# Quantised cross attention: queries on partitions and a turn of the weights, against keys on partitions with four heads at a time

## The chip, the cores and the metric

The kernel runs on one core of a Trainium2 chip. The metric is the device time of one execution in microseconds (us), the median of several runs. Nothing else runs on the core.

## The reference

Four gated layers work on x (2048 rows of 512). Each adds tanh(gate) times a cross attention and tanh(gate) times a feed-forward part. The change is in the attention of the second layer, whose 16 heads of 32 channels let 2048 queries look at 2048 keys:

```python
q = _fq_sym(q * scale, axis=-1)            # steps of max|q| / 127, per row and head
k = _fq_sym(k, axis=-1)
v = _fq_sym(v, axis=2)                     # per channel, over the keys
attn = softmax(einsum('bhqd,bhkd->bhqk', q, k))
s = max(attn over keys) / 255
attn = clip(round(attn / s), 0, 255) * s   # unsigned, per query row
out = einsum('bhqk,bhkd->bhqd', attn, v)
x = x + tanh(g) * (out @ Wp + bp)
```

The largest weight of a row becomes 255, so a kernel needs the largest score of each row before it can round any weight of it. With it, exp(score - top + ln 255) rounded to a whole number is the quantised weight, and the sum of the unrounded exponentials divides the result.

## The kernel before

The program is a row of stages, each a block in which all five engines have an instruction list of their own; a stage ends with a barrier of all engines. PSUM has 8 banks of 128 x 512 f32. TensorE (PE) multiplies, VectorE (DVE), ScalarE (ACT) and GpSimd (POOL) work on tiles, SyncE (SP) issues the DMAs. The second layer's attention is this row of stages in `layer1_xattn`: weights split in two f16 parts, keys projected and quantised (`quantised_heads` with `parts=kT`), values (`quantised_values`), then weights, `transposed_parts` and `quantised_heads` for the queries, `attention_quantised`, and last the output projection: weights (`split_weights`), `transposed_parts` of the output o, and `project_and_add`.

`quantised_heads` has two forms. With `ints` (the queries) it keeps whole numbers in one f16 array and the steps in sq. With `parts` (the keys) it multiplies back by the step (L1307), and ACT (L1331) and POOL (L1319) split the product in a high and a low f16 part; both are turned on PE.

`attention_quantised` goes head by head, 16 tiles of 128 queries each, so 256 tiles. For a tile, PE computes the scores twice. The first time (L1512, four matmuls of 512 keys) only DVE reads them, for the row's largest score (L1617, combined in L1621, made a shift in L1625). The second time (L1505, four matmuls) ACT takes exp with scale and shift, two instructions of 1024 keys, written as 16-bit whole numbers, with their sums (L1586). Queries are on partitions there, but the product with the values needs keys on partitions. So PE turns the weights in 16 pieces (L1517), DVE copies half of them out of PSUM (L1630) and ACT the other half (L1592); the whole numbers are read as f16 bit patterns. Then 16 matmuls of 32 columns give the output (L1525), which DVE copies to o (L1635). POOL divides by the sums once per head (L1496 to L1498). The order on each engine is written by hand; the rings are three deep over tiles.

The attention of the third layer (`attention_clipped`, L2198 to L2297) and of the fourth (`attention_causal`, L2714 to L2933) already work with keys on partitions. PE multiplies keys by queries at 128 x 512, ACT takes exp as f32, and the products with the values (L2212, L2806) and with ones (L2215, L2806) are f32 matmuls of 32 columns. Four of these, at four groups of 32 output partitions, run side by side. In the trace each f32 matmul is two instructions.

## Time and profile before

| | us |
|---|---|
| median of 3 runs | 3355.14 (3348.61 to 3356.6) |
| profiled execution, its own time | 3352.55 |
| its span in the profile | 3350.5 |
| attention stage, first POOL instruction to last | 870.4 to 1794.3 |

| engine | busy us | share of span |
|---|---|---|
| PE | 2675.5 | 80% |
| DVE | 2482.1 | 74% |
| ACT | 1909.9 | 57% |
| POOL | 602.2 | 18% |

The shares are means over stages that have different limits. The attention stage is over a quarter of the span, and in it PE, DVE and ACT are all busy for over nine tenths of the time, while POOL has almost nothing to do. The times of the profiled execution are used for all working; it is 2.6 us below the median of the runs.

### The profile page before, as it was taken

Reading aid. Unit: us, or ns where it says so; the run is one execution under the profiler, and the core shown is the slowest. Engines: PE = TensorE matmul, PEld = TensorE weight load, DVE = VectorE, ACT = ScalarE, POOL = GpSimd, SP = SyncE. Lnnn points to the kernel's source line nnn. Section 1 sums busy time; section 2 is a strip of 40 time slices with the busy share of each in tenths; the row PEclk is TensorE's granted clock in tenths of the full one; section 3 lists DMA queues with packets and bytes.
Section 4 is the critical chain, followed back from the end, with each engine's and each line's share of the span. In section 5 each row is a group of like instructions: output and inputs, shape, how many; then the busy total and the mean of one; then the engine's idle time right before and its main releaser. Section 6 shows DMA issues by size and latency. Waiting matters only on the chain. (4 is left out here: it accounts for less than half of the span.)

```text
span 3350.5 us, 62405 instructions
## 1 busy us (share of the span) xinstructions
PE 2675.5 (80%) x21148; PEld 1391.2 (42%) x21148; DVE 2482.1 (74%) x4757; ACT 1909.9 (57%) x2773; POOL 602.2 (18%) x539
## 2 busy tenths in 40 slices
PE   4868999686799999999996777776698756759983
PEld 3444444333365656565663433333311132224542
DVE  5756677666799999999995666634299798986548
ACT  2554433232499999999995433331387534845541
POOL 4440000012100010101013233312111260030013
PEclk7988999897899999999998888888799877869996
DMA  4433420200000000000000200010133010031301
GB/s 151 174 145 121 151 77 38 91 0 16 19 13 7 13 7 13 7 13 8 7 1 16 88 1 0 0 63 16 44 86 82 26 51 0 1 101 39 66 8 54
DMA packets 65338, 151.98 MB, mean 45 GB/s; under 512 B 11840, under 2 KB 20048, under 8 KB 63376
## 3 DMA queue, kind: packets, MB, share of 16 engines
q1 hardware_dynamic: 62368, 140.43, 14.1%
q0 software_dynamic: 2800, 9.18, 0.8%
q8 instruction: 119, 1.95, 0.2%
q14 instruction: 51, 0.42, 0.0%
HBM read 93.61 MB, written 24.38 MB: 35 GB/s over the span
## 5 line engine op out<-in xcount | busy, mean ns | idle before, releaser
L1617 DVE TENSOR_REDUCE s_top<-ps 128x1 f32<-128x512 f32 x1024 | 656.2, 682 | 30.3 <-PE ps L1512 30.0
L1586 ACT ACTIVATE s_prob<-ps,s_shift,m_sq 128x1024 int16<-128x1024 f32 x512 | 614.7, 1201 | 29.9 <-DVE s_shift L1625 29.9
L1512 PE MATMUL ps<-s_ks,s_qs 128*128 128x512 f16 x1024 | 352.5, 386 | 60.6 <-issue 14.1
L1517 PEld LDWEIGHTS ps<-ident,s_prob 128*128 128x128 f16 x4096 | 272.2, 98 | 123.1 <-DVE m_o L1635 52.3
L1517 PE MATMUL ps<-ident,s_prob 128*128 128x128 f16 x4096 | 313.8, 220 | 0.7 <-ACT s_prob L1586 0.5
L1505 PE MATMUL ps<-s_ks,s_qs 128*128 128x512 f16 x1024 | 306.5, 381 | 0.8 <-ACT s_prob L1586 0.5
L1592 ACT ACTIVATE s_probT<-ps 128x1024 f16<-128x1024 int16 x256 | 261.9, 1023 | 5.8 <-PE ps L1517 4.8
L1008 PE MATMUL ps<-m_hT,m_w 128*128 128x512 f16 x1024 | 231.8, 381 | 1.8 <-PEq L105 1.8
L249 PE MATMUL ps<-ident,s_parts 128*128 128x128 f16 x640 | 75.5, 290 | 130.0 <-POOL s_parts L240 128.1
L2289 DVE TENSOR_SCALAR s_prob<-ps,s_cap 128x1024 f32<-128x1024 f32 x128 | 158.2, 1269 | 25.4 <-PE ps L2198 25.3
L1630 DVE CAST s_probT<-ps 128x1024 f16<-128x1024 int16 x256 | 174.1, 680 | 3.4 <-PE ps L1517 3.4
L2912 DVE TENSOR_REDUCE s_ntop<-ps 128x1 f32<-128x512 f32 (+3 forms) x256 | 107.3, 482 | 87.2 <-PE ps L2772 87.2
L2233 ACT ACTIVATE s_prob<-s_prob 128x1024 f32<-128x1024 f32 x128 | 131.1, 1051 | 58.6 <-DVE s_prob L2289 55.6
L1059 ACT ACTIVATE s_silu<-ps,scale 128x512 f32<-128x512 f32 x64 | 43.9, 685 | 205.3 <-PE ps L1008 205.3
L1496 POOL TENSOR_TENSOR s_sums<-s_z 128x16 f32<-128x16 f32 x16 | 3.5, 217 | 833.5 <-DVE m_o L1635 833.5
L1008 PEld LDWEIGHTS ps<-m_hT,m_w 128*128 128x128 f16 x1024 | 100.5, 98 | 123.8 <-issue 2.2
L1512 PEld LDWEIGHTS ps<-s_ks,s_qs 128*128 (+1 forms) x1024 | 80.4, 96 | 167.5 <-DVE s_top L1617 108.1
L2212 PE MATMUL ps<-s_prob,m_values 128*32 128x512 f32 x512 | 136.0, 610 | 13.0 <-ACT s_prob L2233 12.8
L1525 PE MATMUL ps<-s_hv,s_probT 128*128 128x32 f16 x4096 | 142.2, 176 | 1.7 <-ACT s_probT L1592 1.7
L2883 ACT ACTIVATE s_prob<-ps 128x384 f32<-128x384 f32 (+1 forms) x192 | 89.5, 516 | 86.0 <-PE ps L2795 85.8
L2215 PE MATMUL ps<-s_prob,s_ones 128*32 128x512 f32 x512 | 136.0, 610 | 0.0
L1525 PEld LDWEIGHTS ps<-s_hv,s_probT 128*128 128x128 f16 x4096 | 129.5, 96 | 2.2 <-issue 2.2
(407 smaller groups left out, 5622.4 us busy)
## 6 DMA issues: line engine op xcount, KB each, us to landing
s_qs<-m_qT SPq DMA_DIRECT2D x144, 128.0 KB, 2.5
s_ks<-m_kT SPq DMA_DIRECT2D x96, 128.0 KB, 2.4
numbers<-s_numbers SPq DMA_DIRECT2D x21, 512.0 KB, 3.0
s_slabs<-numbers SPq DMA_DIRECT2D x21, 512.0 KB, 4.4
m_ks<-context_parts SPq DMA_DIRECT2D x12, 512.0 KB, 7.5
expert_rows<-s_y SPq DMA_DIRECT2D x19, 256.0 KB, 2.0
s_rows_in<-in_ctx SPq DMA_DIRECT2D x16, 256.0 KB, 3.0
x_sb<-in_L_ffn_W_up SPq DMA_DIRECT2D x4, 1024.0 KB, 7.2
```

Source lines behind the costliest of these rows:

```text
L1008: i = pe.matmul(k.ps[:, 2 * (n % 2) + j, :], wt[:, c, cols(n, P)], hT[:, l, c, cols(g, GT)], start=(l == c == 0), stop=(l == 1 and c == DC ...
L1505: j = pe.matmul(pair(half)[:, m, :], qs[:, hb, bass.ds(t * P, P)], ks[:, hb, cols(2 * half + m, 512)], start=True, stop=True)
L1512: pe.matmul(quarter_at(q), qs[:, hb, bass.ds(t * P, P)], ks[:, hb, cols(q, 512)], start=True, stop=True).then_inc(s.top_scored, 1)
L1517: j = pe.transpose(turned(half, F16)[:, cols(m, P)], prob[:, u, cols(8 * half + m, P)].bitcast(F16), k.ident[:])
L1525: j = pe.matmul(output, probT[:, u, m, :], hv[:, hb, m, :], start=(m == 0), stop=(m == T - 1))
L1586: act.activation(prob[:, u, cols(half, HALF)], pair(half).rearrange("p m n -> p (m n)"), ACT.Exp, bias=shift[:, u:u + 1], scale=sq[:, bass ...
L1592: act.activation(probT[:, u, 8:16, :].rearrange("p m n -> p (m n)"), turned(1, I16), ACT.Copy).then_inc(s.half1_copied, 1)
L1617: dve.tensor_reduce(top4[:, u, q:q + 1], quarter_at(q), AX.X, ALU.max).then_inc(s.top_read, 1)
L1630: dve.tensor_copy(probT[:, u, 0:8, :].rearrange("p m n -> p (m n)"), turned(0, I16)).then_inc(s.half0_copied, 1)
L2212: pe.matmul(values_at(m)[cols(j, HD), :], values[:, b * KT + t, 2 * pair + j, :], prob[:, n % R, j, :], start=(t == 0), stop=(t == KT - 1))
L2215: i = pe.matmul(sums_at(m)[cols(j, HD), :], ones[:], prob[:, n % R, j, :], start=(t == 0), stop=(t == KT - 1))
L2289: dve.tensor_scalar(prob[:, n % R, :, :], k.ps[:, 2 * (n % A):2 * (n % A) + 2, :], cap[:, tile:tile + 1], -LIMIT, ALU.min, ALU.max).then_i ...
```

## The change

`attention_quantised` is written anew, with keys on partitions. A block is four heads (one 128-partition chunk of the channels) by 512 queries; there are 16 blocks (BLOCKS), each with 16 key tiles (KT) of 128 keys, so 256 steps. In a step, each of the four heads a has:

- one score matmul, 128 keys by 512 queries (`score`, L1574), and one exp of it on ACT, 128 x 512, written as f32 (L1619);
- one cast of these weights to 16-bit whole numbers on POOL (`tensor_copy`, L1528);
- a share of two groups of four 32-column matmuls side by side: values times the whole numbers read as f16 (`mix_values`, L1583), and ones times the f32 weights (`mix_ones`, L1590). Both lag the scores by two steps.

Both groups add up in PSUM over the block's 16 steps, in bank 6 and bank 7. The turning of weights (16 pieces a tile), the copies out of PSUM and the read-outs per tile go.

The largest scores are still taken with queries on partitions: four matmuls a step (`top`, L1557) and four DVE reductions (L1651), 19 steps ahead (AHEAD), in three banks of their own. Since queries are now in the free dimension, the shift can't be a bias of ACT. DVE makes three f16 parts of the least negated top for the block's 16 tiles (L1657 to L1661), PE turns them (L1564), DVE copies them (L1668), and a DMA puts them in 5 more rows of the queries, against 5 rows of 16 in the keys. So the score matmul has 96 + 5 rows. Three DMAs a head load the queries of a block (`queries`, 12 a block) and the keys of four blocks (`keys`). Queries are stored with their step multiplied in and in two parts, as the keys are: `quantised_heads` runs with `parts=qT` for them, three combinations of parts are stacked in the 96 rows, and the separate factor sq goes. Where `quantised_heads` had one multiplication of two tensors (and for queries one more for the scale), it has one scalar_tensor_tensor.

At a block's end ACT copies both sums out (L1625, L1626). SP stores the four rows of sums to DRAM, loads them as 128 rows of 16, DVE inverts those (L1672), and SP stores them and loads them again spread over 32 partitions a head. POOL multiplies (L1533), ACT makes the high part (L1630), POOL the low part (L1537), directly in qT and already in the layout that `project_and_add` reads. So o and the stage `transposed_parts(k, oT, tiles=o)` go. The loops are written out: nothing is a hardware loop in this stage.

On PE, in the middle of the attention stage, a tile before (ks and qs are stacked keys and queries, prob the weights, probT the turned weights, hv a head's values) is:

```order
L1512 MATMUL ps<-s_ks,s_qs 128x512
L1511 REGISTER_ALU
L1512 MATMUL ps<-s_ks,s_qs 128x512
L1533 ISA
L1505 MATMUL ps<-s_ks,s_qs 128x512 x2
L1536 REGISTER_ALU
L1517 MATMUL ps<-ident,s_prob 128x128 x8
L1525 MATMUL ps<-s_hv,s_probT 128x32 x16
```

and the other half of the tile has the same again without the last row. A step now (ints are the whole numbers, ones a tile of one value) is:

```order
L1574 MATMUL ps<-s_qs,s_ks 128x512
L1557 MATMUL ps<-s_ks,s_qs 128x512
L1583 MATMUL ps<-s_ints,m_values 32x512 x4
L1574 MATMUL ps<-s_qs,s_ks 128x512
L1557 MATMUL ps<-s_ks,s_qs 128x512
L1590 MATMUL ps<-s_prob,s_ones 32x512 x4
L1574 MATMUL ps<-s_qs,s_ks 128x512
L1557 MATMUL ps<-s_ks,s_qs 128x512
L1574 MATMUL ps<-s_qs,s_ks 128x512
L1557 MATMUL ps<-s_ks,s_qs 128x512
```

Eight full matmuls remain of eight; 16 turns and 16 matmuls of 32 columns became two groups of four, each entered from a full matmul and left to one.

On DVE, the rows between the reductions of one block and of the next (ntop are the negated tops, compact the sums as 128 rows of 16) are now:

```order
L1651 TENSOR_REDUCE s_ntop<-ps 128x1 x64
L1657 TENSOR_REDUCE s_least<-s_ntop 128x16
L1658 TENSOR_SCALAR s_shift<-s_least 128x16
L1659 SCALAR_TENSOR_TENSOR s_rest<-s_least,s_shift 128x16
L1660 TENSOR_SCALAR s_shift<-s_rest 128x16
L1661 TENSOR_TENSOR s_shift<-s_rest,s_shift 128x16
L1651 TENSOR_REDUCE s_ntop<-ps 128x1 x4
L1668 COPY s_shiftT<-ps 80x128
```

Five dependent small instructions stand between two reductions once a block; before, a small pair stood there once a tile.

On ACT, the copies at a block's end stand behind the exps of the next block's second step:

```order
L1619 ACTIVATE s_prob<-ps 128x512 x72
L1625 ACTIVATE s_sums<-ps 128x512
L1626 ACTIVATE s_num<-ps 128x512
L1619 ACTIVATE s_prob<-ps 128x512 x40
L1630 ACTIVATE m_qT<-s_num 128x512
```

72 exps are 18 steps, so the first copy waits for the last matmul of step 15 with the exps of steps 16 and 17 already ahead of it.

The diff, cut to its core:

```diff
@@ -1292,11 +1292,9 @@
                     v.done(dve.reciprocal(inv[:], step[:, u, :]))
-                    if scale != 1.0:
-                        v.done(dve.tensor_scalar(inv[:], inv[:], scale, None, ALU.mult))
-                    v.done(dve.tensor_tensor(scaled[:, u, :].rearrange("p (h d) -> p h d", d=HD),
-                                             rows[:, u, :].rearrange("p (h d) -> p h d", d=HD),
-                                             inv[:].unsqueeze(2).broadcast_to([P, H, HD]), ALU.mult))
+                    v.done(dve.scalar_tensor_tensor(scaled[:, u, :].rearrange("p (h d) -> p h d", d=HD),
+                                                    rows[:, u, :].rearrange("p (h d) -> p h d", d=HD), scale,
+                                                    inv[:].unsqueeze(2).broadcast_to([P, H, HD]), ALU.mult, ALU.mult))
...
@@ -1416,254 +1414,273 @@
-def attention_quantised(k, qT, sq, kT, values, o):
...
+def attention_quantised(k, qT, kT, values):
...
+    SHIFTS = 5
...
+    A = H // DC
+    ROWS = 3 * HD
...
+    STEPS = BLOCKS * KT
+    TILES = A * TG
+    AHEAD = KT + 3
+    LAG = 2
+    EVACUATE, INVERT, DIVIDE, HIGH, LOW = 1, 6, 9, 11, 11
+    END = STEPS + KT
...
+        qs = s.sb("qs", [P, 3, A, GT], F16)
+        ks = s.sb("ks", [P, 2, A, N], F16)
+        prob = s.sb("prob", [P, 4, A, GT], F32)
+        ints = s.sb("ints", [P, 3, A, GT], I16)
...
+        mixed_at, sums_at = k.ps[:, 6, :], k.ps[:, 7, :]
...
+            def spread_inverse(b):
+                sp.wait_ge(s.evacuated, 2 * b + 1)
+                sp.dma_start(k.inverse[0, :, :], sums[0:P:HD, :]).then_inc(s.sums_stored, 16)
+                sp.wait_ge(s.sums_stored, 16 * (b + 1))
+                sp.dma_start(compact[:], k.inverse[0, :, :].rearrange("a (j e) -> (a j) e", j=HD)).then_inc(s.sums_loaded, 16)
+                sp.wait_ge(s.inverted, b + 1)
+                sp.dma_start(k.inverse[1, :, :].rearrange("a (j e) -> (a j) e", j=HD), compact[:]).then_inc(s.inverse_stored, 16)
+                sp.wait_ge(s.inverse_stored, 16 * (b + 1))
+                for a in range(A):
+                    sp.dma_start(sums[cols(a, HD), :], k.inverse[1, a, :].partition_broadcast(HD)).then_inc(s.inverse_spread, 16)
+            for b in range(BLOCKS):
+                sp.wait_ge(s.top_read, number["shift", b] + 1)
+                sp.dma_start(qs[ROWS:ROWS + SHIFTS, b % 3, :, :], shiftT[:, b % 2, :]).then_inc(shifted[b % 3], 16)
+                if b and b + 2 < BLOCKS:
+                    sp.wait_ge(s.scored, A * KT * b)
+                    for a in range(A):
+                        queries(b + 2, a, q_loaded[(b + 2) % 3])
+                if b and b % G == 0 and b // G + 1 < DC:
+                    for a in range(A):
+                        keys(b // G + 1, a, k_loaded[(b // G + 1) % 2])
+                if b:
+                    spread_inverse(b - 1)
+            spread_inverse(BLOCKS - 1)
...
+            pool.memset(ks[ROWS:ROWS + SHIFTS, :, :, :].rearrange("p u a n -> p (u a n)").bitcast(F32), TWO_SIXTEENS
+                        ).then_inc(s.consts_ready, 1)
+            for n in range(STEPS + KT):
+                if n < STEPS:
+                    if n >= 3:
+                        pool.wait_ge(s.values_mixed, n - 2)
+                    for a in range(A):
+                        pool.wait_ge(s.exp_ready, A * n + a + 1)
+                        pool.tensor_copy(ints[:, n % 3, a, :], prob[:, n % 4, a, :]).then_inc(s.rounded, 1)
+                if n >= KT and n % KT == DIVIDE:
+                    b = n // KT - 1
+                    pool.wait_ge(s.inverse_spread, 16 * A * (b + 1))
+                    pool.wait_ge(s.evacuated, 2 * (b + 1))
+                    pool.tensor_tensor(num[:], num[:], sums[:], ALU.mult).then_inc(s.divided, 1)
+                if n >= KT and n % KT == LOW:
+                    b = n // KT - 1
+                    pool.wait_ge(s.hi_ready, b + 1)
+                    pool.tensor_tensor(qT[:, 1, b // G, cols(b % G, GT)], num[:], qT[:, 0, b // G, cols(b % G, GT)],
+                                       ALU.subtract).then_inc(s.lo_ready, 1)
...
+            def bank_free(job):
+                if job >= 3:
+                    pe.wait_ge(s.top_read, job - 2)
+            def top(i, q):
+                b, a, tile = i // TILES, i % TILES // TG, i % TG
...
+                job = number["top", i, q]
+                bank_free(job)
+                pe.matmul(top_at(job), qs[0:ROWS, b % 3, a, cols(tile, P)], ks[0:ROWS, c % 2, a, cols(q, GT)],
+                          start=True, stop=True).then_inc(s.top_scored, 1)
+            def turn_shift(b):
+                job = number["shift", b]
+                bank_free(job)
+                pe.wait_ge(s.shift_ready, b + 1)
+                pe.transpose(k.ps16[0:SHIFTS * TILES, job % 3, 0:P], shift[:, b % 2, :, :].rearrange("p l i -> p (l i)"),
+                             k.ident[:]).then_inc(s.top_scored, 1)
+            def score(n, a):
+                b, t = n // KT, n % KT
+                g = A * n + a
+                if t == a == 0:
+                    pe.wait_ge(shifted[b % 3], 16 * (b // 3 + 1))
+                if g >= 3:
+                    pe.wait_ge(s.exp_ready, g - 2)
+                pe.matmul(score_at(g), ks[0:ROWS + SHIFTS, b // G % 2, a, cols(t, P)], qs[0:ROWS + SHIFTS, b % 3, a, :],
+                          start=True, stop=True).then_inc(s.scored, 1)
+            def mix_values(n):
+                b, t = n // KT, n % KT
+                if t == 0 and b:
+                    pe.wait_ge(s.evacuated, 2 * b)
+                pe.wait_ge(s.rounded, A * (n + 1))
+                for a in range(A):
+                    j = pe.matmul(mixed_at[cols(a, HD), :], values[:, t, cols(b // G * A + a, HD)],
+                                  ints[:, n % 3, a, :].bitcast(F16), start=(t == 0), stop=(t == KT - 1))
+                j.then_inc(s.values_mixed, 1)
+            def mix_ones(n):
+                t = n % KT
+                for a in range(A):
+                    j = pe.matmul(sums_at[cols(a, HD), :], ones[:], prob[:, n % 4, a, :],
+                                  start=(t == 0), stop=(t == KT - 1))
+            for m in range(-AHEAD, END):
+                i = m + AHEAD
...
+                for a in range(A):
+                    if 0 <= m + 1 < STEPS:
+                        score(m + 1, a)
+                    if i < STEPS:
+                        top(i, a)
+                    if a == 0 and LAG <= m < STEPS + LAG:
+                        mix_values(m - LAG)
+                    if a == 1 and LAG <= m < STEPS + LAG:
+                        mix_ones(m - LAG)
+                if i % TILES == 0 and 0 < i <= STEPS:
+                    turn_shift(i // TILES - 1)
...
+            def exp(n, a):
+                g = A * n + a
+                if a == 0 and n >= 4:
+                    act.wait_ge(s.mixed, n - 3)
+                act.wait_ge(s.scored, g + 1)
+                act.activation(prob[:, n % 4, a, :], score_at(g), ACT.Exp).then_inc(s.exp_ready, 1)
+            def evacuate(b):
+                if b:
+                    act.wait_ge(s.lo_ready, b)
+                act.wait_ge(s.mixed, KT * (b + 1))
+                act.activation(sums[:], sums_at, ACT.Copy).then_inc(s.evacuated, 1)
+                act.activation(num[:], mixed_at, ACT.Copy).then_inc(s.evacuated, 1)
+            def hi(b):
+                act.wait_ge(s.divided, b + 1)
+                act.activation(qT[:, 0, b // G, cols(b % G, GT)], num[:], ACT.Copy).then_inc(s.hi_ready, 1)
...
+            for n in range(STEPS + KT):
+                if n < STEPS:
+                    for a in range(A):
+                        exp(n, a)
+                if n >= KT and n % KT == EVACUATE:
+                    evacuate(n // KT - 1)
+                if n >= KT and n % KT == HIGH:
+                    hi(n // KT - 1)
...
+            def tops(i):
+                b = i // TILES
+                for q in range(4):
+                    job = number["top", i, q]
+                    dve.wait_ge(s.top_scored, job + 1)
+                    dve.tensor_reduce(ntop[:, b % 2, i % TILES, q:q + 1], top_at(job), AX.X, ALU.max, negate=True
+                                      ).then_inc(s.top_read, 1)
+            def shifts(b):
+                dve.wait_ge(s.top_read, number["top", TILES * (b + 1) - 1, 3] + 1)
+                hi, mid, lo = (shift[:, b % 2, r, :] for r in range(3))
+                v.done(dve.tensor_reduce(least[:], ntop[:, b % 2, :, :], AX.X, ALU.min))
+                v.done(dve.tensor_scalar(hi, least[:], 1.0 / SIXTEEN, None, ALU.mult))
+                v.done(dve.scalar_tensor_tensor(rest[:], least[:], 1.0 / SIXTEEN, hi, ALU.mult, ALU.subtract))
+                v.done(dve.tensor_scalar(mid, rest[:], 1.0, None, ALU.mult))
+                dve.tensor_tensor(lo, rest[:], mid, ALU.subtract).then_inc(s.shift_ready, 1)
+            def copy_shift(b):
+                job = number["shift", b]
+                if b >= 2:
...
+                dve.wait_ge(s.top_scored, job + 1)
+                dve.tensor_copy(shiftT[:, b % 2, :], k.ps16[0:SHIFTS * TILES, job % 3, 0:P]).then_inc(s.top_read, 1)
+            def invert(b):
+                dve.wait_ge(s.sums_loaded, 16 * (b + 1))
+                dve.reciprocal(compact[:], compact[:]).then_inc(s.inverted, 1)
+            for m in range(-AHEAD, END):
+                i = m + AHEAD
+                if i < STEPS:
+                    tops(i)
+                if i % TILES == 0 and 0 < i <= STEPS:
+                    copy_shift(i // TILES - 1)
+                if i % TILES == TILES - 1 and i < STEPS:
+                    shifts(i // TILES)
+                if m >= KT and m % KT == INVERT:
+                    invert(m // KT - 1)
...
@@ -3096,15 +3113,12 @@
...
             transposed_parts(k, hT, taken=True)
-            quantised_heads(k, hT, wq, k.i.L1_xattn_bq, scale, sq=sq[:].rearrange("p (h t) -> p t h", t=T), ints=qT)
-        o = sb("o", [P, H, T, HD], F32)
-        attention_quantised(k, qT, sq, kT, values, o)
+            quantised_heads(k, hT, wq, k.i.L1_xattn_bq, scale, parts=qT)
+        attention_quantised(k, qT, kT, values)
...
-            oT = sb2("oT", [P, 2, DC, N], F16)
             split_weights(k, k.i.L1_xattn_Wp, wp, row_factor=sv)
-            transposed_parts(k, oT, tiles=o)
-            project_and_add(k, oT, wp, k.i.L1_xattn_bp, 1)
+            project_and_add(k, qT, wp, k.i.L1_xattn_bp, 1)
...
```

## Rows read from the trace of the kernel before

**Rows 1.** Busy by engine in four stretches (from:to, length, PE, PEld, DVE, ACT, POOL, clock).
```profile
870.40:1794.40 924.00, 856.81 (x10240) 545.95 (x10240) 875.81 (x2048) 882.78 (x1281) 86.87 (x67) 0.98 0.04 10
807.50:869.70 62.20, 52.51 (x256) 23.18 (x256) 50.05 (x128) 9.55 (x16) 0.00 (x0) 0.91 0.01 5
639.60:714.60 75.00, 54.54 (x320) 26.14 (x320) 62.41 (x112) 24.78 (x32) 18.44 (x16) 0.93 0.05 18
1806.20:1828.20 22.00, 11.58 (x128) 8.47 (x129) 11.06 (x16) 9.74 (x16) 17.76 (x16) 0.81 0.00 0
```

**Rows 2.** Groups by line and form, 880 to 1795 us.
```profile
L1617 DVE TENSOR_REDUCE s_top<-ps 128x1 f32<-128x512 f32 x1024 | 656.2, 682 | 30.3 <-PE ps L1512 30.0
```

**Rows 3.** Instructions in order of time, PE, one tile of the attention.
```profile
1300.00 0.89 PE L1512 MATMUL ps<-s_ks,s_qs 128*128 128x512 f16 x2
...
1303.45 0.89 PE L1512 MATMUL ps<-s_ks,s_qs 128*128 128x512 f16 x2
```

**Rows 4.** In order of time, PE, third layer's attention: one step.
```profile
2560.02 0.60 PE L2198 MATMUL ps<-s_qs,s_ks 128*128 128x512 f16 x2
2560.55 0.62 PE L2212 MATMUL ps<-s_prob,m_values 128*32 128x512 f32 x2
...
2561.01 0.60 PE L2212 MATMUL ps<-s_prob,m_values 128*32 128x512 f32 x2
...
2561.55 0.60 PE L2198 MATMUL ps<-s_qs,s_ks 128*128 128x512 f16 x2
```

**Rows 5.** In order of time, PE, query projection: twelve full matmuls in a row.
```profile
818.32 2.75 PE L1247 MATMUL ps<-m_wq,m_hT 128*128 128x512 f16 x12
```

**Rows 6.** In order of time, PE, fourth layer: a narrow f16 matmul between.
```profile
3144.45 0.28 PE L2806 MATMUL ps<-s_prob,s_ones 128*32 128x128 f32 x2
3144.59 0.22 PE L2777 MATMUL ps<-ident,s_shift 128*16 128x128 f16 x1
3144.74 0.39 PE L2792 MATMUL ps<-s_qs,m_ks 98*128 98x512 f16 x1
```

**Rows 7.** Groups by line and form, POOL, whole span.
```profile
L2274 POOL TENSOR_TENSOR s_out<-s_num,s_inv 128x512 f32<-128x512 f32 x16 | 20.3, 1269 | 126.0 <-DVE s_inv L2297 125.9
...
L2276 POOL TENSOR_TENSOR m_qT<-s_out,m_qT 128x512 f16<-128x512 f32 x16 | 18.6, 1161 | 79.2 <-ACT m_qT L2247 79.2
...
L1488 POOL COPY s_hv<-m_values 128x512 f16<-128x512 f16 x16 | 9.7, 609 | 1.0
...
L142 POOL CAST ident<-ident 128x128 f16<-128x128 f32 x1 | 0.3, 289 | 0.1
```

**Rows 8.** Groups by line and form, ACT, whole span.
```profile
L2883 ACT ACTIVATE s_prob<-ps 128x512 f32<-128x512 f32 x64 | 33.7, 572 | 0.5 <-PE ps L2795 0.4
...
L2241 ACT ACTIVATE s_sums<-ps 64x512 f32<-64x512 f32 x32 | 19.0, 593 | 2.1 <-PE ps L2215 1.3
```

**Rows 9.** In order of time, DVE and POOL, the last key tile of quantised_heads.
```profile
707.14 1.15 POOL L1319 TENSOR_TENSOR s_f<-s_rows,s_f 128x512 f16<-128x512 f32 x1 [2.97 <-ACT s_f L1331]
707.76 0.57 DVE L1291 TENSOR_SCALAR s_step<-s_amax 128x16 f32<-128x16 f32 x1
```

**Rows 10.** The same view, DVE, the last query tile.
```profile
866.36 0.17 DVE L1291 TENSOR_SCALAR s_step<-s_amax 128x16 f32<-128x16 f32 x1
```

**Rows 11.** Groups by line and form, DVE, whole span.
```profile
L1716 DVE SCALAR_TENSOR_TENSOR x_sb<-ps,gate,x_sb 128x512 f32<-128x512 f32 x16 | 12.0, 751 | 23.4 <-PE ps L1686 23.4
...
L1297 DVE TENSOR_TENSOR s_scaled<-s_rows,s_inv 128x512 f32<-128x512 f32 x32 | 22.1, 692 | 1.2
```

**Rows 12.** In order of time, start and end of the attention stage.
```profile
870.41 5.21 POOL L1479 MEMSET s_qs<- 64x6144 f16 x1 [65.71 <-POOLq L105]
...
881.87 1.01 PE L1512 MATMUL ps<-s_ks,s_qs 128*128 128x512 f16 x2 [12.82 <-POOL s_hv L1488]
...
1793.28 1.05 POOL L1498 TENSOR_TENSOR m_o<-m_o,s_sums 128x512 f32<-128x512 f32 x1
```

**Rows 13.** DMA issues by line in the attention stage (KB each, us from issue to landing).
```profile
s_qs<-m_qT SPq DMA_DIRECT2D x32, 128.0 KB, 2.3
```

259 lines of the change are left out of this document (66 added, 193 removed).

## The prediction, before the changed kernel was run

> **What bounds the kernel now.** I read the busy time by stretch first. The attention stage takes 924.0 us, and PE is busy for 857, DVE for 876 and ACT for 883 of them, POOL for 87 [rows 1]. Three engines are level, so taking work from one alone would buy little. What counts is the longest engine of the new step. Next I read the instructions in order of time in mid-stage: one tile starts 3.45 us after the one before it [rows 3], and 924.0 / 256 is 3.61 with start, head changes and end. Last I looked for the new instructions where other stages already have them: the third layer's attention has full matmuls beside groups of four narrow f32 ones [rows 4], the fourth has a narrow f16 matmul [rows 6] and the 512-wide exp [rows 8].
>
> **One step on PE.** Twelve full matmuls in a row take 2.75 us, of which the last one's own latency is 0.39 [rows 5, 6], so (2.75 - 0.39) / 11 = 0.2145 us each. Eight of them, four scores and four for the tops: 1.72. In the third layer a step of two full matmuls and one f32 group of four repeats every 2561.55 - 2560.02 = 1.53 us [rows 4]. Less 0.43 for the two full ones, the group costs 1.10: 0.10 to enter, two instructions a member 0.46 apart, and the rest to leave. That is `mix_ones`. `mix_values` has f16 operands, thus one instruction a member. No row shows four narrow f16 matmuls side by side. From below: hidden switches, 0.21. From above: members one after another with both switches, 4 x 0.21 + 0.20 = 1.06. The nearest row is the narrow f16 transpose of 128 columns. It starts 0.14 us after the last f32 narrow pass, but the full matmul behind it starts 0.15 us after it, although 128 columns take only 0.054 [rows 6]. So leaving the narrow shape costs 0.10 with f16 too, and I take 0.10 + 0.21 + 0.10 = 0.42. The sum is 1.72 + 1.10 + 0.42 = 3.24 us a step on PE.
>
> The Trainium skill, TensorEngine Tiling (Array Packing), Key Properties, says that changing the tiling mode drains the engine. This case's trace agrees, with its 0.10 us on either side of a narrow group. It speaks against this change, which changes the shape four times a step where a tile before never did; by it the narrow f16 group is 0.42, not 0.21.
>
> **The other engines in a step.** DVE: 1024 reductions take 656.2 us [rows 2], 0.641 each, four are 2.56. ACT: four exps of 0.572 [rows 8] are 2.29; two copies of 0.593 and one of about 0.6 a block add 0.11: 2.40. POOL: the cast from f32 to 16-bit whole numbers is in no row. A f16 copy of 512 takes 0.609 and a f32 to f16 cast of 128 takes 0.289 [rows 7]; one slope of 0.83 ns an element and 0.18 us fixed fit both, so I take 0.61. Four are 2.44, and the multiplication (1.27) and the low part (1.16) of a block [rows 7] add 0.15: 2.59. From below 0.5 (an overlap of instructions); from above the two-input price, 1.27 [rows 7], which would make a POOL step of 5.2. PE at 3.24 is the longest, so POOL and ACT work is hidden beside it. If the cast takes over 0.77, POOL sets the step.
>
> The Trainium skill, GPSIMD Engine Reference, section 3.1, gives 769 ns measured as the best case for 512 elements of a tight loop. The 0.609 row is below that, so the measurement decides; by the page POOL would have 3.08 + 0.15 = 3.23 a step, level with PE, and the time would hardly move.
>
> **The whole stage.** PE's first matmul now waits for POOL's memset of 8192 elements a partition. 6144 took 5.21 us [rows 12], so 6.95, and with small ones before it PE starts at 870.4 + 7.5 = 877.9, four us sooner than the 881.9 of before [rows 12].
>
> - Prologue: 19 steps hold only top matmuls. DVE is the longest there: 76 x 0.641 = 48.7, plus some 1.9 for the first shift's chain: 928.5. PE and ACT can't use this time; before there was no such stretch.
> - 237 steps with tops: two without mixing at DVE's 2.57, 235 at 3.24: 766.5.
> - ACT at a block's end. The copies stand behind the exps of the second step after it and wait for `mixed` of step 15, which PE ends 2.46 us into that step (after four full matmuls and the f16 group come two passes of 0.46 and a latency of 0.60). ACT has been free since 1.8 us before. It copies for 1.11 us and only then takes the exps again. Three score banks absorb three matmuls; the fourth, due at 2.83 into the step, needs the first exp done, 2.5 + 1.15 + 0.6 = 4.25. PE stands for 1.4 us, and as it is the longest engine, that is lost: 15 blocks, 21 us.
> - DVE at a block's end: five dependent instructions. At 0.17 us for a small one [rows 10] with some 0.04 between, they take 1.1. But while POOL's two-input instruction ran, the same small one took 0.57 instead of 0.17 and ended with POOL's [rows 9, 10]. Now POOL is busy for four fifths of the time, so each of four may wait up to 0.6: 3.0 at most. The rings hide 1.2 of it. I take 2.3, a stall of 1.1 x 15 = 16 us (from 0 to 28). The turn of the shift adds 15 x 0.15 = 2.
> - 18 steps without tops at 3.24 - 0.86 = 2.38 and three with mixing only at 1.52: 47.4.
> - The end, where nothing covers the scratch chain: a copy 0.6, then store, load, inversion some 0.25 (a small DVE instruction takes 0.17 [rows 10]), store and four spreading DMAs; four landings at 2.3 [rows 13] and three more issues of 0.6 are 11.0; then 1.27, 0.6 and 1.16. Together 15.3. In the other 15 blocks POOL asks for the spread sums eight steps (26 us) after the copy. The chain has some 16 us of work, its DVE instruction stands at step 6, and POOL's casts run over one step ahead of their use, so I cost it at nothing. Behind the waits stand SP's next loads, due 13 steps into the block.
>
> 928.5 + 766.5 + 21 + 16 + 2 + 47.4 + 15.3 = 1796.7. With 2 us for PE's clock, which may have to rise after the thin prologue, 1798.7, where the stage before ended at 1794.3 [rows 12]: +4.4 us.
>
> **Around the stage.** The queries' `quantised_heads` now has the form of the keys'. It took 62.2 us for the queries and 75.0 for the keys [rows 1]: +12.8. The multiplication becomes a scalar_tensor_tensor, 0.751 in the nearest row (one operand in PSUM) against 0.692 [rows 11], 32 times: +1.9 at most, between 0 and that. The `transposed_parts` of o goes, 22.0 us with its barrier [rows 1]; a barrier remains, so -20.9. The projection then starts after an idle PE instead of after turns: +2 for its clock. Sum: 4.4 + 12.8 + 1.8 - 20.9 + 2 = +0.1.
>
> The profiled execution took 3352.55 us; 3352.6 on its scale, and since the median of the runs lies 2.6 above it, 3355.3. For code written out, whose loading no row prices at a stall, I add one: **3356 us**. So large a rewrite ends near zero, because the saving per step, 3.45 - 3.24 = 0.2 us or 54 us in all, is given back by the prologue and the stalls at each block's end.
>
> **Rivals.**
> 1. The step is shorter: the narrow f16 group costs 0.21 (its switches merge or its loads are hidden), which is 0.2 x 238 = 50 us less, or DVE's five instructions wait for nothing, 16 less. About 3300. For it: rows show four f32 members side by side without loss. Against: 0.10 in rows 6 for f16.
> 2. Slower, by POOL: a cast to whole numbers at 0.95 us makes a step of 3.8 + 0.15 and some 0.6 x 256, about 3500. It decides from 0.77 us on. For it: every POOL instruction that does arithmetic costs over twice the copy. Against: the f32 cast of 128 lies on the copy's line.
> 3. Slower, by block ends: DVE's five wait fully for POOL, the copies' stall is 2.5 instead of 1.4 and the spread sums come late to POOL, 15 x 3 = 45 more: 3400. For it: all of PE's waits are in one order, and nothing is ever caught up. Against: the slack worked out above.
> 4. The f16 members don't run side by side: +0.64 a step, about 3510. Against it: rows 4, where the f32 ones do.
>
> **How the numbers follow.** A measurement of this kernel can tell a change from none from about 0.3% on, 10 us. My forecast has 0.48, with its own range of 3335 to 3385; of that 0.14 lies below 3345, 0.22 within, 0.12 above 3365. Rival 1 has 0.20, rival 2 0.15, rival 3 0.13, rival 4 0.04. Faster 0.34, same 0.22, slower 0.44. The range of 3300 to 3470 leaves out the lower half of rival 1 and the far part of 2 and 4.
>
> **What would show it.** PE's steps in mid-stage 3.24 us apart, with a full matmul 0.4 us behind each f16 group's start; DVE waiting for PE in each step; POOL's casts at 0.61 and ahead of PE; about 50 us at the start with PE mostly idle; once a block a PE wait for an exp behind ACT's two copies, 1.4 us, and one for a DVE reduction, about 1 us; the queries' stage at 75 us. PE waiting for a cast in mid-block would make rival 2 right and the forecast wrong; steps of 3.0 us would make rival 1 right.

## The result and the profile after

The changed kernel takes 3358.97 us (median of 20 runs, 3353.59 to 3364.19), the kernel before 3351.61 us (20 runs, 3347.99 to 3357.62). The ratio is 1.0019, 95% interval 1.0012 to 1.0026. The change costs 7.4 us, 0.2%, inside the 0.3% that was called no change; 3356 had been forecast. Run once more in another batch, the changed kernel took 3360.06 us, 1.0026 (1.0017 to 1.0036) of before, and the kernel before against itself was 1.0001 (0.9992 to 1.0010). So the small loss is real.

The profiled execution took 3358.79 us, its span is 3356.9. First the stretches, in the columns of [rows 1]: the attention stage, its first part, the same stage well inside, and the queries' projection.

```profile
880.30:1816.80 936.50, 882.60 (x5136) 225.32 (x5136) 670.08 (x1136) 578.52 (x1073) 640.56 (x1060) 0.96 0.08 20
884.00:928.00 44.00, 39.34 (x67) 6.95 (x67) 39.62 (x70) 0.00 (x0) 3.51 (x1) 0.50 0.41 94
1000.00:1700.00 700.00, 675.76 (x4069) 175.38 (x4067) 530.97 (x898) 457.37 (x849) 502.72 (x838) 1.00 0.07 18
807.50:882.00 74.50, 52.22 (x315) 25.10 (x313) 62.39 (x112) 26.08 (x33) 20.11 (x20) 0.94 0.00 1
```

The columns are the stretch, its length, the busy time of PE, PEld (PE's weight loads), DVE, ACT and POOL with the numbers of instructions, and last PE's granted clock, the DMA share and GB/s. The first row answers to the first of [rows 1]. DVE has fallen from 876 to 670 us and ACT from 883 to 579, POOL has risen from 87 to 641, and PE, which was level with the others, is now alone in front with 883 of 936.5. The second row is the prologue, the stretch before the first score: PE's matmuls for the tops run at a granted clock of 0.50 (the 1.2 GHz level), and PE waits for DVE. In the third the clock is 1.00, and PE is busy for 676 of 700 us. The fourth answers to the other rows of [rows 1]: the queries' projection now keeps DVE busy for 62.4 us, as the keys' did before.

One step of PE in order of time (start, length, engine, line, operation); these answer to [rows 3 to 5]:

```profile
1252.01 0.39 PE L1574 MATMUL ps<-s_qs,s_ks 101*128 101x512 f16 x1
1252.23 0.38 PE L1557 MATMUL ps<-s_ks,s_qs 96*128 96x512 f16 x1
1252.55 1.06 PE L1590 MATMUL ps<-s_prob,s_ones 128*32 128x512 f32 x8
1253.54 0.39 PE L1574 MATMUL ps<-s_qs,s_ks 101*128 101x512 f16 x1
...
1254.65 0.38 PE L1557 MATMUL ps<-s_ks,s_qs 96*128 96x512 f16 x1
1254.95 0.40 PE L1583 MATMUL ps<-s_ints,m_values 128*32 128x512 f16 x4
1255.29 0.39 PE L1574 MATMUL ps<-s_qs,s_ks 101*128 101x512 f16 x1
```

From L1574 at 1252.01 to L1574 at 1255.29 it is 3.28 us, and there is no idle time in brackets: PE waits for nobody. Between 1253.54 and 1254.65 lie five spacings, 0.222 each. From the full matmul at 1254.65 to the next at 1255.29 it is 0.64, so the f16 group adds 0.42. From 1252.23 to 1253.54 it is 1.31, so the f32 group adds 1.09. 8 x 0.222 + 0.42 + 1.09 = 3.29.

Two places of a block cost most. The first is the end of a block, where ACT waits for the last f32 group and copies:

```profile
993.38 1.06 PE L1590 MATMUL ps<-s_prob,s_ones 128*32 128x512 f32 x8
...
994.51 0.60 ACT L1625 ACTIVATE s_sums<-ps 128x512 f32<-128x512 f32 x1 [1.90 <-PE ps L1590]
995.00 0.59 ACT L1626 ACTIVATE s_num<-ps 128x512 f32<-128x512 f32 x1
995.48 3.05 ACT L1619 ACTIVATE s_prob<-ps 128x512 f32<-128x512 f32 x6
...
996.14 0.39 PE L1574 MATMUL ps<-s_qs,s_ks 101*128 101x512 f16 x1 [1.16 <-ACT s_prob L1619]
```

ACT has been idle for 1.90 us when the group ends, and copies from 994.51 to about 995.5. Only then does it read scores again. TensorE has three banks for them, so a score matmul finds none free and waits until 996.14. The second is where DVE makes the shift of the block to come:

```profile
1255.51 0.22 DVE L1657 TENSOR_REDUCE s_least<-s_ntop 128x16 f32<-128x64 f32 x1
1255.77 0.63 DVE L1658 TENSOR_SCALAR s_shift<-s_least 128x16 f16<-128x16 f32 x1
1256.43 0.58 DVE L1659 SCALAR_TENSOR_TENSOR s_rest<-s_least,s_shift 128x16 f32<-128x16 f32 x1
1257.05 0.17 DVE L1660 TENSOR_SCALAR s_shift<-s_rest 128x16 f16<-128x16 f32 x1
1257.26 0.18 DVE L1661 TENSOR_TENSOR s_shift<-s_rest,s_shift 128x16 f16<-128x16 f32 x1
...
1258.09 0.39 PE L1557 MATMUL ps<-s_ks,s_qs 96*128 96x512 f16 x1 [0.44 <-DVE s_ntop L1651]
1258.68 0.25 PE L1564 MATMUL ps<-ident,s_shift 128*80 128x128 f16 x1 [0.20 <-DVE s_ntop L1651]
```

The waits of the stage, grouped (who <- for whom: us in total, times, longest), show both, and a small third one, that of the shift's turn (L1564):

```profile
PE ps L1574 <- ACT s_prob L1619: 18.4, 15, 1.4
...
PE ps L1557 <- DVE s_ntop L1651: 7.5, 16, 1.1
PE ps L1564 <- DVE s_ntop L1651: 2.9, 14, 0.2
...
PE ps L1583 <- POOL s_ints L1528: 0.6, 1, 0.6
```

A column of idle time understates a stall here, because a matmul's modelled end reaches over the next start. The distance between the copies of two blocks is the better measure. Those at L1625 start 55.45 us apart (median of the first 13 distances, 55.39 to 55.50): 16 steps of 3.28 are 52.48, so a block's end costs 2.97 us. The distances from one step's first score to the next step's tell where: 4.70 us at ACT's copies, 4.34 at DVE's shift and 3.77 at the turn behind it (means over the blocks), thus 1.42, 1.06 and 0.49 over 3.28.

### The profile page after: what moved, and what is told of

It is laid out like the page before. It is cut to its first block and busy times, and to the rows that moved or that the text cites. A ratio compares the mean times of both kernels' runs of the same rounds, so it can differ in the third digit from the quotient of the medians.

```text
span 3356.9 us, 46711 instructions
## 1 busy us (share of the span) xinstructions
PE 2690.2 (80%) x15980; PEld 1063.6 (32%) x15980; DVE 2277.4 (68%) x3813; ACT 1611.4 (48%) x2565; POOL 1157.1 (34%) x1532
## 5 line engine op out<-in xcount | busy, mean ns | idle before, releaser
L1651 DVE TENSOR_REDUCE s_ntop<-ps 128x1 f32<-128x512 f32 x1024 | 641.2, 682 | 208.8 <-PE ps L1557 206.7
L1619 ACT ACTIVATE s_prob<-ps 128x512 f32<-128x512 f32 x1024 | 554.9, 600 | 315.7 <-PE ps L1574 314.8
L1528 POOL CAST s_ints<-s_prob 128x512 int16<-128x512 f32 x1024 | 597.4, 618 | 284.7 <-ACT s_prob L1619 266.4
L1557 PE MATMUL ps<-s_ks,s_qs 96*128 96x512 f16 x1024 | 406.0, 398 | 18.7 <-POOL s_ks L1520 9.1
L1574 PE MATMUL ps<-s_qs,s_ks 101*128 101x512 f16 x1024 | 390.9, 387 | 20.7 <-ACT s_prob L1619 18.4
L1590 PE MATMUL ps<-s_prob,s_ones 128*32 128x512 f32 x2048 | 272.6, 604 | 0.0
L1574 PEld LDWEIGHTS ps<-s_qs,s_ks 101*128 101x128 f16 x1024 | 98.7, 98 | 364.6 <-ACT s_prob L1619 284.1
L1984 POOL TENSOR_TENSOR s_weighted<-s_hid,s_lnw 128x512 f32<-128x512 f32 x64 | 94.3, 1475 | 159.9 <-DVE s_hid L1996 159.9
L1557 PEld LDWEIGHTS ps<-s_ks,s_qs 96*128 96x128 f16 x1024 | 101.3, 99 | 115.8 <-DVE s_ntop L1651 53.6
L2232 PE MATMUL ps<-s_prob,s_ones 128*32 128x512 f32 x512 | 135.2, 607 | 0.0
L2900 ACT ACTIVATE s_prob<-ps 128x384 f32<-128x384 f32 (+1 forms) x192 | 89.6, 516 | 85.8 <-PE ps L2812 85.7
L1019 PE MATMUL ps<-m_w,s_hid 128*128 128x512 f16 x512 | 120.9, 379 | 5.9 <-DVE s_hid L1164 5.9
```

What stands on the lines that cost most here:

```text
L1019: i = pe.matmul(k.ps[:, YB + t, :], hid[:, n % Q, l, cols(t, P)], w.down[:, n, :], start=(n == l == 0), stop=(n == FC - 1 and l == 1))
L1528: pool.tensor_copy(ints[:, n % 3, a, :], prob[:, n % 4, a, :]).then_inc(s.rounded, 1)
L1557: pe.matmul(top_at(job), qs[0:ROWS, b % 3, a, cols(tile, P)], ks[0:ROWS, c % 2, a, cols(q, GT)], start=True, stop=True).then_inc(s.top_sco ...
L1574: pe.matmul(score_at(g), ks[0:ROWS + SHIFTS, b // G % 2, a, cols(t, P)], qs[0:ROWS + SHIFTS, b % 3, a, :], start=True, stop=True).then_inc ...
L1590: j = pe.matmul(sums_at[cols(a, HD), :], ones[:], prob[:, n % 4, a, :], start=(t == 0), stop=(t == KT - 1))
L1619: act.activation(prob[:, n % 4, a, :], score_at(g), ACT.Exp).then_inc(s.exp_ready, 1)
```

## The experiments

All changes are to the changed kernel unless it is said otherwise; "block" is the distance between the copies of two blocks' sums in mid-stage, 55.45 us in the changed kernel. Differences are between medians, against 3359.0. The kernel before had medians of 3351.2, 3354.9 and 3351.8 us beside the runs of three groups (the first four experiments; the three together, the pairs, the fifth cast and the pause in the kernel before; the rest), so a difference of 3 to 4 us between groups tells nothing.

**One narrow stretch a step instead of two.**

```diff
-                    if a == 0 and LAG <= m < STEPS + LAG:
-                        mix_values(m - LAG)
                     if a == 1 and LAG <= m < STEPS + LAG:
+                        mix_values(m - LAG)
                         mix_ones(m - LAG)
```

> The two groups of the mixing matmuls of a step (four over values, in f16; four over ones, in f32) are issued directly behind each other, so that a step has one stretch of narrow matmuls instead of two. Nothing is left out. Theory A (each passage from 96-row or 101-row matmuls to the 32-column ones and back costs the time of the drain, 0.10 us each way, as the spacings 0.31 and 0.33 around the f16 group show beside 0.215 for plain neighbours): two passages of four go, a step of 3.28 falls to 3.08 or so, and with 237 to 256 steps the kernel takes 45 to 50 us less than the changed one, some 3311; the four matmuls of the f16 group then cost little more than one plain one. Theory B (the cost belongs to each group, or to the change of type between f16 and f32, not to the passage): the change from f16 to f32 now stands between the groups and costs the same, 0 to 25 us less, 3334 to 3359. Against both, if POOL's cast is what the step waits for (its wait now stands at the second score of a step), the step stays at 3.28 or grows: 3359 or more.

Measured: 3308.36 us, 0.9870 (0.9855 to 0.9885) of before: -50.6. The step in its trace:

```profile
1249.99 0.38 PE L1557 MATMUL ps<-s_ks,s_qs 96*128 96x512 f16 x1
1250.30 0.40 PE L1583 MATMUL ps<-s_ints,m_values 128*32 128x512 f16 x4
1250.53 1.03 PE L1590 MATMUL ps<-s_prob,s_ones 128*32 128x512 f32 x8
1251.49 0.39 PE L1574 MATMUL ps<-s_qs,s_ks 101*128 101x512 f16 x1
```

Entering still costs 0.31 - 0.22 = 0.09. From the f16 to the f32 group it is 0.23, no more than between plain neighbours, although the type changes. So theory A holds: the passage between shapes costs, not the group or the type. The step is 3.04 us, -0.24; two passages are thus 0.12 each. A block is 52.05, -3.40 where 16 x 0.24 is 3.8: 0.4 is given back at the block's end. Why a passage costs is not separated. In both traces the weight load of the first matmul behind a passage is recorded together with that matmul (1254.95 and 1250.30), while between full neighbours it starts one matmul ahead, about 0.22 us, and from the f16 to the f32 group 0.21 ahead. A drain of the engine and a load of 0.10 us that can't run ahead would both look like this.

**ACT's copies between its second and third exponential.**

```diff
+                for a in range(A):
+                    if n >= KT and n % KT == EVACUATE and a == 2:
+                        evacuate(n // KT - 1)      # EVACUATE is 2 instead of 1
```

> ACT's two copies at a block's end (sums and mixed rows, 15 times inside the loop) are issued between the second and the third exponential of the next step instead of behind a whole step. Nothing is left out. Theory A (in the changed kernel ACT waits 1.9 us for the last f32 group of the block, and its next exponential is so late that TensorE stands about 1.4 us for a bank of scores, 15 times): the copies no longer wait for the group, the exponentials stay ahead, and about 1.4 x 15 = 21 us go: some 3338. Rival (the stall is the reductions' of the same block end, or is given back by them): 0 to 5 us less, 3354 to 3359.

Measured: 3336.20 us, 0.9956 (0.9942 to 0.9969): -22.8. A block is 54.09, -1.36, the 1.4 of the forecast, and the row of PE's waits for ACT's exponentials in the list of waits is gone. Theory A holds.

**The sums inverted where they lie, without the scratch.** VectorE's reciprocal takes `sums[:]` (128 x 512) instead of `compact[:]`, and `spread_inverse` with its DMAs is not called.

> The sums are inverted by VectorE as they lie (128 x 512, one reciprocal a block), without the six DMAs and the scratch in DRAM. Nothing else is changed. Theory A (VectorE has little to spare and TensorE waits for its reductions: it is busy 2.6 of 3.28 us a step, so a reciprocal of 3.34 us, as the third layer's of this shape takes, delays the reductions by some 2 us more than the three banks cover, 15 times, while the chain behind the last block loses about 5 us of DMAs and waits and gains the 3.3 of the reciprocal): 25 to 30 us slower than the changed kernel, some 3386. Rival B (the reductions catch up in the slack of 0.7 us a step, and the reordered waits cover the rest): 3359 within 5. Rival C (the DMAs disturb the loads of queries and the scratch costs more than it shows): 5 to 10 us faster, 3350.

Measured: 3392.24 us, 1.0121 (1.0106 to 1.0137): +33.3. The groups by line and form, stage only:

```profile
L1669 DVE RECIPROCAL s_sums<-s_sums 128x512 f32<-128x512 f32 x13 | 43.4, 3342 | 0.0
```

The reciprocal that took 0.24 us on 128 x 16 takes 3.34. Blocks are 57.45 or 58.9 us, 2.0 or 3.4 more. The 2.0 are the delayed reductions; in the five blocks of 58.9 us, and only in those, the granted clock is besides 0.5 for 3.4 us, which costs 1.4. From the first copies to those of the last block it is 35.3 longer in all, and the chain at the end gives 4.9 back, so the stage is 30.4 longer; the rest of the 33 is not assigned. Theory A holds, a little above its number: the scratch in DRAM is worth some 30 us.

**The shift's operations between the reductions.**

```diff
                     dve.tensor_reduce(ntop[...], top_at(job), ...).then_inc(s.top_read, 1)
+                    if i % TILES == 0 and i:
+                        shift_part(b - 1, q + 1)   # one of the four behind each reduction
```

(AHEAD is KT + 4, and the turn and its copy stand at `i % TILES == 1`.)

> The five small operations of VectorE that make a block's shift stand one by one behind the four reductions of the next step instead of all five in a row, and the turn of the shift and its copy come one step later, for which the reductions run one step further ahead (20 steps instead of 19 in the part before the first score). Nothing is left out. Theory A (the five take 1.84 us in a row, since each waits for the one before, and TensorE stands about 1.1 us for a bank behind them, 15 times): 16 us go, and the longer part at the beginning adds 2.6 for the twentieth step of reductions but takes it from the later part, net +1 to +2: 14 us less, some 3345. Rival B (the reductions stand in the same step anyway, four waits of 0.4 us instead of one of 1.8, and the three banks cover neither): 0 to 3 us less, 3356 to 3361.

Measured: 3345.22 us, 0.9978 (0.9969 to 0.9987): -13.8, where 14 was expected. A block is 54.42, -1.03. The step with the turn stays at 3.74. Theory A holds.

**The three edits together.**

> The three edits together: the two mixing groups adjacent, ACT's copies between the second and third exponential, the shift's small operations between the reductions. Nothing is left out. Theory A (three separate stalls, each removed once): by the single runs -50.6, -22.8 and -13.8 against 3359.0, so 3272. Rival B (in the faster step of 3.03 us the casts and exponentials are close behind, and the first edit alone already showed waits for POOL and ACT; part of what is removed comes back as a wait for another engine): 3280 to 3290.

Measured: 3280.59 us, 0.9780 (0.9767 to 0.9794): -78.4, and 74 below the kernel before in the same batch. This version beats both. A block is 49.91, -5.54 where the three single edits sum to -5.79, so only 0.25 a block comes back, 4 us in all. The three single runs sum to -87.2, so the median is at the lower end of B's 3280 to 3290. Counted from the kernel before as it ran beside each, with the changed one 7.4 above it, the three together are 81.7 below the changed kernel and the single ones sum to 85.8. So part comes back, as B has it, but only some 4 us.

**The mixing of two steps in one stretch.**

```diff
+                    if a == 1 and m % 2 == 0 and LAG <= m < STEPS + LAG:
+                        mix_values(m - 2)
+                        mix_values(m - 1)
+                        mix_ones(m - 2)
+                        mix_ones(m - 1)
```

> As the three together, but the mixing of two steps is issued in one stretch every second step (values, values, ones, ones), so that there is one narrow stretch for sixteen wide matmuls. Nothing is left out. Theory A (a passage costs about 0.12 us whatever is in between): another 0.12 to 0.25 us a step on average, 30 to 60 us less than the three together, 3220 to 3240. Rival B (the stretch is then over 2.3 us long, more than the three banks of scores and the three of tops hold for ACT and VectorE, so that these starve in it and TensorE waits for them afterwards): the same as the three together within 10, or slower.

Measured: 3351.41 us, 0.9990 (0.9981 to 0.9999): 71 slower than the three together. In order of time, without the weight loads, two steps:

```profile
1280.32 4.88 DVE L1652 TENSOR_REDUCE s_ntop<-ps 128x1 f32<-128x512 f32 x8 [1.49 <-PE ps L1557]
...
1282.86 0.39 PE L1557 MATMUL ps<-s_ks,s_qs 96*128 96x512 f16 x1
1283.09 0.38 PE L1574 MATMUL ps<-s_qs,s_ks 101*128 101x512 f16 x1
1283.46 0.39 PE L1557 MATMUL ps<-s_ks,s_qs 96*128 96x512 f16 x1
1283.78 0.61 PE L1583 MATMUL ps<-s_ints,m_values 128*32 128x512 f16 x8
1284.22 1.89 PE L1590 MATMUL ps<-s_prob,s_ones 128*32 128x512 f32 x16
```

Before the narrow stretch the tops' matmuls come 0.60 us apart, at DVE's pace: eight reductions are 4.88 us, and 1.49 us DVE stands idle because three banks don't last through a stretch of 2.3 us. Two steps are 4.88 + 1.49 = 6.37 instead of 6.08. Rival B holds: the banks run dry. But 8 x 0.29 is only 2.3 of the 4.7 us by which a block is longer (54.65 in mid-stage). In ten of the blocks the granted clock is 0.5 for 3.4 us, and those without it take 53.0, so the clock costs 1.6 more. (It is 0.93 in four of the eight stretches of 25 us from 1200 to 1400.) The rest is at the block's end.

**A fifth cast on POOL.** `pool.tensor_copy(spare[:], prob[:, n % 4, 0, :])` before the third cast of each step.

> POOL makes a fifth cast in each step, of a tile already cast, into a tile that nobody reads; the rest is the changed kernel. It measures how much room POOL has. By the rows of the changed kernel four casts are 2.47 of a step of 3.28 us, five 3.09, so that with two more operations a block POOL still fits. Theory A (POOL is hidden as long as its sum is under the step): 3359 within 5. Rival B (TensorE's wait for the fourth cast binds already by its latency, since the mixing of a step waits for casts of the step before it but two): 0.3 us or more a step, 3430 or more.

Measured: 3427.91 us, 1.0218 (1.0204 to 1.0232): +68.9. The size is that of rival B, but its reason was wrong. In mid-block the steps are still 3.28 us apart, so POOL has its room there. Blocks are 59.0 or 60.3 us, 3.6 or 4.9 more, and the loss is at one place, the steps with the shift and its turn:

```profile
1335.05 2.30 POOL L1533 CAST s_ints<-s_prob 128x512 int16<-128x512 f32 x4
...
1335.21 2.16 DVE L1663 TENSOR_SCALAR s_shift<-s_least 128x16 f16<-128x16 f32 x1
...
1337.41 0.58 DVE L1664 SCALAR_TENSOR_TENSOR s_rest<-s_least,s_shift 128x16 f32<-128x16 f32 x1
...
1339.77 0.39 PE L1562 MATMUL ps<-s_ks,s_qs 96*128 96x512 f16 x1 [2.68 <-DVE s_ntop L1656]
```

An operation of 0.17 us takes 2.16 and ends with POOL's fourth cast. The three behind it took 0.58, 0.53 and 0.52, though POOL went on with its casts. PE stands for 2.68 us instead of 0.44, which is 2.2 of the loss, and its granted clock is 0.51 for the next seven (1340 to 1347). The rest of the loss goes with the clock: all of these blocks have 3.4 or 6.8 us at 0.5, the longer ones 6.8.

The Trainium skill, SBUF — State Buffer, section on the two sides, says that DVE and GpSimd share a pair of ports under an exclusive lock, held for a whole instruction. The trace agrees that one waits for the other, but this wait reaches over four of POOL's instructions. That the port is the cause follows from the page and from the end of the wait; no run here tests another cause.

**The same with a pause for that place.** The fifth cast is left out in two of sixteen steps: `if a == 2 and n % KT not in (13, 14)`.

> As the kernel with five casts, but the fifth is left out in two of a block's sixteen steps, those in which VectorE makes the shift. In the trace of the five casts the steps stay at 3.28 us; what is new is that one small f16 operation of the shift (128 x 16) took 2.16 us instead of 0.63 while POOL ran four casts without a gap, TensorE then stood 2.68 us and its granted clock fell for some microseconds. Theory A (VectorE's f16 operation and POOL's casts exclude each other at a port, and the operation gets in only when POOL pauses; all of the 69 us hang on that one place, 16 times): with pauses at that place the kernel is back near 3359, at most 15 above. Rival B (the loss is POOL's total: four casts more or less a block don't matter): two eighths of it at most go, 3410 or more.

Measured: 3385.89 us, 1.0106 (1.0091 to 1.0122): +26.9. Neither number was hit, but B is out: 12% fewer of the extra casts removed some 60% of the loss. The pause came too late. In order of time, with POOL's casts before and behind:

```profile
1316.00 3.98 POOL L1533 CAST s_ints<-s_prob 128x512 int16<-128x512 f32 x7
...
1318.40 1.60 DVE L1663 TENSOR_SCALAR s_shift<-s_least 128x16 f16<-128x16 f32 x1
...
1320.04 0.18 DVE L1664 SCALAR_TENSOR_TENSOR s_rest<-s_least,s_shift 128x16 f32<-128x16 f32 x1
...
1320.54 1.18 POOL L1533 CAST s_ints<-s_prob 128x512 int16<-128x512 f32 x2 [0.57 <-ACT s_prob L1624]
...
1321.29 0.39 PE L1562 MATMUL ps<-s_ks,s_qs 96*128 96x512 f16 x1 [1.01 <-DVE s_ntop L1656]
```

The first operation still waits for the end of a row of seven casts (1.60 us in 14 blocks of 16), the following ones are back at 0.17 to 0.18 since POOL pauses, and PE stands for 1.01 us instead of 2.68. Against the changed kernel's 0.44 that is 0.6 a block, and blocks of 56.0 us have just this; in eight of thirteen the granted clock is 0.5 for 3.4 us behind the wait, and they take 57.4.

**A pause in the kernel before, and one in the changed.** VectorE fills and inverts a spare tile (0.27 + 1.75 = 2.0 us, and 0.48 + 3.35 = 3.8) before the last projection of the layer may start.

> The kernel before, with 2 us more of waiting at the start of the layer's last projection (VectorE fills a spare tile and inverts it, 256 columns, before it lets TensorE start); all stages behind it are unchanged. It tells where 5 of the 7 us of the changed kernel's median are: in its trace the layer itself ends 1.4 us late, and the distance grows to 6.2 us in later stages in which both kernels are the same. Theory A (what follows takes a few us more or less by how it lies to the changes of TensorE's granted clock, so a delay is not passed on one to one): the total rises by clearly more or less than 2, such as -3 or +7, against 3351.2. Rival B (the extra time is work of the change after all, or of the chip): 3353, by the 2 us.

> The changed kernel with about 3.7 us more of waiting at the start of the layer's last projection (VectorE fills and inverts a spare tile of 512 columns before it lets TensorE start). The counterpart of the same pause in the kernel before, which cost 3.2 us for 2. Theory A (stages behind it take more or less by how they lie to changes of the granted clock): clearly off 3.7, such as 0 or +8, against 3359. Rival B: 3362 to 3364, by the pause alone.

Measured: 3358.07 us for the first, 1.0009 (1.0000 to 1.0018) of before, 3.2 more than the 3354.88 in its batch; 3362.05 for the second, 3.1 more than 3359.0 and 2.0 more than the changed kernel beside it (3360.06). Medians of 8 to 11 runs can't tell 2 from 4 us here (the first has an interval of 0 to 6), so that a delay is passed on one to one is compatible with both and not shown. Theory A's several us more or less did not appear.

**Both kernels once more.**

> The changed kernel once more, unchanged, for a second trace and as a measure of what a repetition moves. Expected: 3359 within 2, and 1.0019 of the time before within 0.0007. If the 5 us by which its later, unchanged stages were longer are a matter of the single execution, they lie elsewhere in this trace or are gone while the median stays; if they belong to the kernel, they are there again behind 2229 us.

> The kernel before once more, unchanged, against its own earlier runs: 1.000 within 0.001. Its second trace tells how far two executions of the same kernel lie apart in the stages behind the layer: theory A (granted clock, by execution) 2 to 6 us at single places; rival B (the stages take the same time to 1 us).

Measured: 3360.06 and 3352.75 us. Both repeated within what was expected, to 1.1 us. The second traces place the difference. Each span cut at three instructions that both kernels have (the ones that start the split of `Wkv`, the attention stage, the last projection):

| trace | up to the split | to the attention stage | attention and turning | projection to end |
|---|---|---|---|---|
| before | 632.4 | 238.0 | 957.8 | 1522.3 |
| before, again | 633.7 | 236.4 | 960.0 | 1518.2 |
| changed | 631.4 | 248.9 | 949.9 | 1526.7 |
| changed, again | 631.5 | 251.2 | 951.7 | 1522.9 |

The segments of one kernel differ by up to 4 us between its two traces, as theory A of the last expectation has it. The heads (the projections and quantising of keys and queries) cost +12.9 us on average, attention with the turning of its output -8.1, what is behind +4.6, and what is ahead, with no difference in code, -1.6. The last column is the same code apart from the projection's source. In the nine other traces of versions of the changed kernel, it is between 1521.3 and 1528.8, so 7 us lie between traces there, and what belongs to the change in it can't be told from four traces. Against the first trace of the kernel before, the first of the changed kernel is 1.2 us late where the layer has ended (1889) and 6.2 at the end; this growth was not there in the second, which is 6.5 us late at that point and 6.8 at the end.

## Why the prediction was right

- **The step on PE** was forecast at 3.24 and is 3.28. Groups were exact: 0.42 forecast and measured for f16, 1.10 and 1.09 for f32. The 0.04 is in the eight full matmuls, which start 0.222 apart rather than 0.2145. Over 235 steps it is 9 us. The first experiment showed that the 0.42 was right for its reason: 0.1 on either side of a narrow stretch, and four f16 members side by side like one. So rival 4 fell, and rival 1 with its group of 0.21.
- **POOL's cast** takes 0.618 us (1024 of them), for 0.61 forecast from the line through a copy and a short cast. Rival 2 fell: the loop holds one wait of PE for a cast, of 0.6 us.
- **ACT's copies** were forecast to cost 1.4 a block and cost 1.36, as taking their wait away showed. The whole chain of reasons (ACT free 1.9 us, three banks absorbed, the fourth late) is in the rows.
- **DVE's five** took 1.84 us instead of 2.3, since only two of the four wait for POOL (0.63 and 0.58) and the other two fit into its pause. Their stall was forecast at 1.1 a block; taking it away gave 1.03. That it is so close is luck in part: the five were 0.5 shorter than forecast, and the banks hid only 0.8 of them (1.84 less 1.06) where 1.2 had been taken. The other half of rival 1, that the five wait for nothing, fell with the 0.63 and 0.58. With the turn's 0.15 the forecast for a block's end was 2.65, measured 2.97: the difference is the turn, whose step is 0.49 longer, not 0.15, since the turn too waits for a bank of the tops. Rival 3, with 3 us more, fell.
- **The stage** is 936.5 us where 928.3 follows from the forecast, 8.2 more. By its terms: the prologue -5.6 (52.5 from the stage's start to the first score instead of 58.1, as 64 reductions that wait for nothing took 38.35 us there, 0.60 each where 0.641 was taken from a sum of busy time), full matmuls +9.4, block ends +4.8, the chain at the end -3.2 (12.1 instead of 15.3: four landings of 1.4 to 2.1 where 2.3 was taken; besides, the forecast's own parts add up to 14.9). That is +5.4; the clock's rise behind the prologue costs more than the 2 taken, since the first fourteen from 932.8 on are 0.43 apart instead of 0.22, and the rest of the 8.2 is not assigned.
- **Around it** the errors go the other way. The queries' stage with the keys' was forecast at +12.8 + 1.8. The scalar_tensor_tensor takes 0.692 us, as the multiplication did, not the 0.751 of a row with an operand in PSUM, so the 1.8 is nil; the measured segment is +12.9, or +11.9 if all 14 traces are taken in. The turning went as forecast: -20.5 for -20.9.
- Sum: -8 for attention and turning where -16.5 was forecast, +12 to +13 where +14.6, and +2.5 to +4.6 behind, where 3 was: between +6 and +9, and 7.4 was measured against 0.9 forecast (3356 against a median of 3355.1). No run separates the 2 us for the projection's clock and the 1 us for written-out code; their 3 lies in the same segment. The forecast of no large effect stood because the two sides of the sum were both read from rows. That it came within 7 us is luck in part, since errors of -5.6, +9.4, +4.8 and -3.2 cancel in part. **The term that was mis-sized** is the stage, by 8 us of 936, and its largest part is the spacing of the full matmuls, an error of 3% in a number that counts 1880 times. I had taken it from matmuls of 128 rows that follow one another on one line [rows 5]; those of two alternating lines with their own weights are 0.222 apart.
- What the forecast had of cover was right: the seven DMAs of the scratch (the expectation above says six) are hidden in 15 of 16 blocks (POOL waited once for the spread sums, 10.4 us, at the end), and their alternative on DVE made the stage 30 longer.

The gain per step, 3.45 - 3.28 = 0.17 us or 43 us in all, is given back by the prologue (45 us in which PE runs at half clock for DVE, against 0.88 saved in each of the 18 last steps), block ends (15 x 2.97) and the longer heads. It was not lost for good: another order of the same instructions gave 78 us.

## What to carry to other kernels

Count a switch between full and narrow matmuls like an instruction, and put all narrow groups of a step behind each other, but no longer than the banks of the engines it feeds last. Where an in-order engine has to take a value that comes late in a step, put its instruction as late as its readers allow, in the middle of its other work rather than behind it; the moves of ACT's copies and of DVE's chain each gave just the stall that the rows had shown. Ask also what a stall does to the clock: where it fell behind one, that cost 1.4 us or more on top. A term multiplied by two thousand deserves a spacing read to three digits from the shape at hand.
